# An fp32 operand buffer re-laid so that four batch rows interleave per feature slot, in a DLRM interaction tower

## The reference

```
e = jnp.stack([tbl_0[ids[:, 0]], ..., tbl_25[ids[:, 25]]], axis=1)          # 512 x 26 x 128
combined = jnp.concatenate([dense[:, None, :], e], axis=1)                  # 512 x 27 x 128
interactions = jnp.einsum('bfd,bgd->bfg', combined, combined)
z = concatenate([dense, interactions[:, iu, ju]], axis=1)                   # iu < ju
h = concatenate([z, dense], axis=1)                                         # 607 wide
h = maximum(h @ W_top1 + b_top1, 0);  h = maximum(h @ W_top2 + b_top2, 0);  y = h @ W_top3
```

## Time and profile before

| | |
|---|---|
| median of 3 runs | 181.42 us (180.19 to 184.68) |
| span of the profiled execution | 181.4 us; its own time is not listed apart from the runs |
| mean granted TensorE clock | 0.802 |
| PE / PEld busy | 115.4 us (64%) / 98.3 us (54%) |
| DVE / ACT / POOL busy | 71.7 (40%) / 71.9 (40%) / 79.6 us (44%) |
| DMA | 12.67 MB, mean 70 GB/s |

### The profile page before, as it was taken

One profiled execution on the slowest core, in us unless ns is written; L12 is line 12 of the kernel. 1 busy time (PEld: TensorE's weight loads), 2 busy tenths in 40 slices (PEclk: granted clock), 3 DMA queues, 4 the chain that ended last, 5 costly groups with the idle time before them and its releaser, 6 DMA issues.

```text
span 181.4 us, 1866 instructions
## 1 busy us (share of the span) xinstructions
PE 115.4 (64%) x694; PEld 98.3 (54%) x694; DVE 71.7 (40%) x119; ACT 71.9 (40%) x112; POOL 79.6 (44%) x84
## 2 busy tenths in 40 slices
PE   6177746952814000099889571398785959797795
PEld 6164525832603000078789461197685957797692
DVE  4173476632320011186294400265624643164430
ACT  0465098545042000378664400235541462265422
POOL 1777777777777776073787777000000000000000
PEclk9858975996575555558999955558999999999999
DMA  4956456859831121010112121000000000000000
GB/s 90 260 173 192 150 170 172 186 188 241 251 120 44 44 58 43 14 47 18 54 29 59 46 58 52 20 0 0 4 0 0 0 0 4 0 0 4 0 0 0
DMA packets 5738, 12.67 MB, mean 70 GB/s; under 512 B 1849, under 2 KB 2361, under 8 KB 5602
## 3 DMA queue, kind: packets, MB, share of 16 engines
q1 hardware_dynamic: 3010, 7.26, 13.6%
q0 software_dynamic: 2432, 4.99, 10.3%
q10 hardware_dynamic: 288, 0.32, 0.9%
HBM read 12.55 MB, written 0.00 MB: 69 GB/s over the span
## 4 chain that ended last, share of the span: by engine, by line
PE 46%; another core or an unknown queue 22%; issue 9%; DVE 9%; DMA 7%; ACT 6%; SPq 1%; ACTq 0%; DVEq 0%
PE gram L416 14%; PE late L386 8%; DMA table<-in_tbl 7%; PE late L387 7%; PE gram L432 3%; DVE dots L564 3%; PE look L396 3%; PE late L450 2%; DVE onehot L729 2%; PE late L452 2%; PE late L451 2%; PE look L488 1%; DVE w_lo L803 1%; ACT table_hi L587 1%
## 5 line engine op out<-in xcount | busy, mean ns | idle before, releaser
L341 POOL DMA_INDIRECT e_rows<-in_tbl,idx x76 | 78.8, 1036 | 33.4 <-issue 22.6
L386 PE MATMUL late<-onehot,table_hi 125*128 125x512 f32 x56 | 29.1, 519 | 41.3 <-DVE onehot L729 21.6
L416 PE MATMUL gram<-eT 128*123 128x104 f32 x256 | 35.1, 298 | 11.3 <-issue 8.4
L416 PEld LDWEIGHTS gram<-eT 128*123 128x123 f32 x256 | 33.2, 213 | 12.8 <-issue 9.4
L386 PEld LDWEIGHTS late<-onehot,table_hi 125*128 125x128 f32 x56 | 14.0, 250 | 47.5 <-ACT eT L587 26.1
L729 DVE TENSOR_SCALAR onehot<-ids,row_of_partition 125x512 fp32r<-125x512 int32 x42 | 19.3, 497 | 36.7 <-remote 23.6
L587 ACT ACTIVATE dots<-gram 32x208 f32<-32x208 f32 x32 | 16.5, 517 | 35.3 <-PE gram L416 20.0
L564 DVE COPY dots<-gram 32x208 f32<-32x208 f32 (+1 forms) x32 | 16.5, 516 | 28.7 <-remote 14.9
L387 PE MATMUL late<-onehot,table_lo 125*128 125x512 f32 x56 | 27.2, 486 | 0.0
L607 ACT ACTIVATE onehot<-distance 125x512 fp32r<-125x512 f32 x14 | 8.8, 631 | 27.2 <-remote 24.3
L556 DVE COPY eT<-look 128x512 f32<-128x512 f32 (+1 forms) x12 | 11.7, 972 | 10.8 <-PE look L396 7.5
(11 more groups left out here) (49 smaller groups left out, 109.1 us busy)
## 6 DMA issues: line engine op xcount, KB each, us to landing
table<-in_tbl SPq DMA_DIRECT2D x6, 500.0 KB
ids<-in_ids_bcast SPq DMA_DIRECT2D x6, 256.0 KB
w_raw<-in_w SPq DMA_DIRECT2D x1, 1280.0 KB
e_rows<-in_tbl,idx POOLq DMA_INDIRECT x76
w_raw<-in_w SPq DMA_DIRECT2D x1, 512.0 KB
table<-in_tbl SPq DMA_DIRECT2D x2, 250.0 KB
ids<-in_ids_bcast ACTq DMA_DIRECT2D x1, 256.0 KB
x_rows<-in_dense SPq DMA_DIRECT2D x1, 256.0 KB
```

The costliest lines, as they stand in the source:

```text
L341: pool.indirect_dma_start(out=e_rows[:, t % 2, s, :], out_offset=None, in_=tables[f][:, :], in_offset=bass.IndirectOffsetOnAxis(ap=idx[:, ...
L386: pe.matmul(bank, table_hi[0:KP, i % 2, c, :], hot, start=c == 0, stop=False)
L416: last = pe.matmul(gram[0:ROWS_OUT, n % 2, q, 0:QUADS * NG_COL], eT_flat[:, b * SLOTS:b * SLOTS + ROWS_OUT], eT[:, b:b + QUADS, 0:NG_COL], ...
```

## The change

`eT` becomes [128, 32 blocks of 16 batch rows, 4, 32 slots, 4]. Batch row 16a + 4j + r, slot s, lies at [a, j, s, r]: for one slot, four batch rows are neighbours, and slots are 16 bytes apart. A copy into eT writes four numbers in a row (16 bytes) and then goes on 512 bytes further; before it wrote one number every 128 bytes. A gram product takes the rows with one r out of a block of 16, so its weights and its moving columns are read one number every 16 bytes; before the weights were one run of 123 numbers and the moving operand four runs of 26. Number, shapes and types of all matmuls and copies stay, as do all waits and all DMAs. The four rows of a product are now 4 apart in the batch, and so `turned` writes `pT_hi` and `pT_lo` in runs of four numbers instead of one number every 16 bytes.

```
+RUN = 4
...
-        eT = sb("eT", [P, B, SLOTS])
+        eT = sb("eT", [P, B // 16, QUADS, SLOTS, RUN])
...
-        eT_flat = eT[:, :, :].rearrange("d b s -> d (b s)")
+        eT_run = eT[:, :, :, :, :].rearrange("d g j s r -> d g (j s) r")
...
-                        b = t * P + (c * CHUNK_Q + q) * QUADS
+                        a, r = divmod(t * Q + c * CHUNK_Q + q, RUN)
                         last = pe.matmul(gram[0:ROWS_OUT, n % 2, q, 0:QUADS * NG_COL],
-                                         eT_flat[:, b * SLOTS:b * SLOTS + ROWS_OUT],
-                                         eT[:, b:b + QUADS, 0:NG_COL], start=True, stop=True)
+                                         eT_run[:, a, 0:ROWS_OUT, r],
+                                         eT[:, a, :, 0:NG_COL, r], start=True, stop=True)
...
-            copy(eT[:, t * P:(t + 1) * P, s:s + n].rearrange("d b f -> d f b"),
-                 look[:, LOOK[what] % 2, 0:n * P].rearrange("d (f b) -> d f b", f=n)).then_inc(done, 1)
+            copy(eT[:, t * 8:(t + 1) * 8, :, s:s + n, :].rearrange("d g j f r -> d f (g j) r"),
+                 look[:, LOOK[what] % 2, 0:n * P].rearrange("d (f q r) -> d f q r", f=n, r=RUN)).then_inc(done, 1)
...
-            return [src] + [t[:, k, :].rearrange("p (q j) -> p j q", j=QUADS) for t in (pT_hi, pT_lo)]
+            src = src.rearrange("p j (g r) -> p j g r", r=RUN)
+            return [src] + [t[:, k, :].rearrange("p (g j r) -> p j g r", j=QUADS, r=RUN) for t in (pT_hi, pT_lo)]
...
-                copy(eT[:, :, 1 + NG + i], late[:, LATE["table", i] % 2, :]).then_inc(late_act, 1)
+                copy(eT[:, :, :, 1 + NG + i, :].rearrange("d g j r -> d (g j) r"),
+                     late[:, LATE["table", i] % 2, :].rearrange("d (q r) -> d q r", r=RUN)).then_inc(late_act, 1)
...
-                    copy(eT[:, :, 0], bank)
+                    copy(eT[:, :, :, 0, :].rearrange("d g j r -> d (g j) r"), bank.rearrange("d (q r) -> d q r", r=RUN))
...
-            dve.memset(eT[:, :, NF:SLOTS], 0.0).then_inc(pads_ready, 1)
+            dve.memset(eT[:, :, :, NF:SLOTS, :].rearrange("d g j s r -> d (g j) (s r)"), 0.0).then_inc(pads_ready, 1)
```

## The result

The changed kernel takes **197.42 us** (median of 4 runs, 195.71 to 201.88) against 180.85 (4 runs, 180.19 to 184.68): ratio **1.089**, 95% interval 1.079 to 1.099, so slower by about 16 us. The forecast was 194.1, the range 178 to 203.

The account below looks back on a forecast made before the run. Up to 117 us a stall with slack, not TensorE, was taken to set the time; after it PE's work and hand-overs. 181.4 + 14.9 for strided reads - 2.2 for faster copies = 194.1 us, range 178 to 203.

Parts of the forecast that it names:

- The price of the strided read: Gram passes: PE pays 1.75 ns per number read 16 bytes apart, so 0.222 us a pass, +0.111 at full clock.
- Separate ports, the longer operand sets the pass: Gram passes: weights and moving columns load through separate ports, so 123 weights, not 104 columns, set the time.
- The same rule for neighbours: Gram passes before the change: 123 neighbouring weights at 0.85 ns plus 7 ns give 0.111 us a pass.
- Tiles 2 and 3: Gram tiles 2 and 3, 64 passes each, all on the path: +6.9 and +7.1 us.
- The copies: Copies into eT, pT_hi and pT_lo, after 117 us: writing runs of four goes at neighbours' pace, -2.2 us.
- the cover before 117 us: Stretch to 117 us: its slack hides 96 longer passes of tile 0 and half of tile 1, costed at nothing.
- the sign of being wrong altogether: Before 117 us: a stall that moves by more than 5 us with PE's place in it.
- its sign of being right: Gram tile 1: its second half still starts near 117 us.
- a rival of its own: Stages behind gram tiles: the slower pass lowers PE's clock, so they start cold, up to +8.7 us; chance 0.17.
- its likeliest case: Whole kernel: the forecast's own case, 194.1 us, range 190 to 199, chance 0.40.
- Rival 1: Gram passes: PE's port hides the stride, passes stay 0.111 us, kernel 179.2 us, between 177 and 181.4; chance 0.32.
- The row that spoke against it: Layer-1 passes: fp32r columns at 0.47 ns, 1.9 ns per 16 bytes, no faster than one 16-byte piece in 1.75 ns.

Follow-up runs that it names:

- the series of steps: Kernels whose gram operands are both read at steps of 4, 8, 12, 16 or 32 bytes: 0.111, 0.117, 0.171, 0.230 and 0.235 us a pass.
- reads_tiles01: Kernel before, both gram operands read one number every 16 bytes in gram tiles 0 and 1 only: 186.78 us against 183.33, ratio 1.049.
- weights_run: Changed kernel, but gram weights alone read as neighbours, moving columns still 16 bytes apart: 190.62 us, one run.
- run2: Changed kernel with two batch rows interleaved instead of four: 180.51 us against 182.07 for the kernel before, ratio 0.994; again 178.93 against 180.93, ratio 0.997.
- slot_inner: Kernel before, group copies into eT writing 16 bytes in a row and jumping in PSUM: 177.91 us against 183.33, ratio 0.997; again 178.95 against 180.93, 1.004.
- reads_tiles23: Kernel before, both gram operands read one number every 16 bytes in gram tiles 2 and 3 only: 197.80 us against 183.33, ratio 1.110.

## Why the prediction held, point by point

- **The price of the strided read**, the step on which all hung, was bounded between no extra at all (0.111 us a pass) and 0.40, and taken at 0.222, from strided writes of DVE. It is 0.230 (1.81 ns a number against 1.75). That reads of PE pay about what writes of DVE pay was an argument then; the series of steps shows the price for PE. That it is one and the same limit of the buffer is still only an inference from equal numbers.
- **Separate ports, the longer operand sets the pass**: shown for strided operands by the two kernels with one of them, 0.190 and 0.228 against 0.192 and 0.226. With a shared port each of the two would lie well below the pass in which both are strided (0.230). The same rule for neighbours, 0.85 ns for each of 123 weights, hit 0.111 us but is not shown: the rows had 128 weights in 0.061 us, and the prediction used both numbers. Nothing in the sum hung on it, since the 0.111 us was measured.
- **Tiles 2 and 3**: +6.9 and +7.1 forecast, +7.7 and +7.6 measured, all on the path.
- **The copies**: -2.2 forecast, -2.2 in the changed kernel's chain (1.0, 0.7 and 0.5 in the three places, where 1.0, 0.7 and 0.4 were forecast), -2.1 alone.
- **Mis-sized: the cover before 117 us.** I costed tile 0 and the first half of tile 1 at nothing and the second half at +0.9. The end of tile 1 came 4.2 us later. That much of the loss is covered was right, since the 128 passes alone would be 15 us, but the stall is no fixed wall at 117 us. In the changed kernel ACT and DVE were released at 111.6 instead of 117.0, and then all 64 passes of tile 1 followed at 0.23 us. That is a move of 5.3 us, past the 5 us that the prediction itself had named as the sign of being wrong altogether; its sign of being right, the second half of tile 1 starting near 117 us, failed as well (121.64). The prediction had the stall end with the DMA traffic. In these rows its end goes with a mere pause of POOL's gathers:

```profile
109.69 0.94 POOL L342 DMA_INDIRECT e_rows<-in_tbl,idx  x1 [0.30 <-issue]
111.62 1.03 ACT L589 ACTIVATE dots<-gram 32x208 f32<-32x208 f32 x2 [8.28 <-remote]
113.05 0.56 DVE L557 COPY eT<-look 128x384 f32<-128x384 f32 x1 [0.40 <-remote]
113.28 0.94 POOL L342 DMA_INDIRECT e_rows<-in_tbl,idx  x1 [2.65 <-remote]
```

  In the changed kernel ACT restarts in a gap between two gathers (1.9 us after the start of the one, DMA share down from 0.37 to 0.03 at that moment), DVE's last copy into eT for tile 1 follows, and PE starts 0.1 us behind it, while three more gathers are still to come. In the kernel before the last gather of all starts at 112.84, and ACT restarts at 116.96; in `reads_tiles01` it restarts at 109.00, in a gap from 103.03 to 109.97. Other profiles also have releases amid running gathers (`weights_run` at 103.62), so this is a pattern and not a cause. What the stall is waiting for stays open: no row names it, and its end lies elsewhere in each profile (the transposes behind tile 1 start between 119.9 and 125.9 us in kernels whose passes in tiles 0 and 1 are those of before). It is probably also what makes totals of this kernel scatter: between the two profiles of `run2`'s kernel the start of those transposes differs by 2.3 us, of `slot_inner`'s by 4.8, and the stretch from there to the end by 1.6 and 0.8.
- **Mis-sized: the clock.** It had a rival of its own (0.17, up to +8.7), which came half true. During strided tiles the clock can be at either level: in the changed kernel 17 passes fill 3.9 us at 0.50 and 3.8 us at 1.00,

```profile
113.70:117.60 3.90, 3.89 (x17) 3.90 (x18) 0.50 0.18 49
...
167.20:171.00 3.80, 3.75 (x17) 3.78 (x17) 1.00 0.00 0
```

  so the gram itself hardly cares, as the rival said. But work behind it sometimes runs at 1.2 GHz: +1.4 us in the changed kernel, +4 in `reads_tiles23`. The stage behind tile 1 was at full clock in the changed kernel. The forecast left the clock out of its likeliest case.
- **The total.** +12.7 was forecast. The two profiled executions differ by 18.7, and the missing 6.0 are the cover (+3.3), the size of a pass (+1.3) and the clock (+1.4), all of the same sign. The medians differ by 16.6, as both profiled executions were longer than their medians, by 4.5 and some 2.3 us (an estimate). How near the total came, 194.1 to 197.4, is in part luck: the stall alone moves it by more than that. The prediction also called the span of the profile equal to the median of the runs; the execution of that profile was about 183.2 us long, and the two figures agree by chance. And the range, 178 to 203, reached from no change at all to the slowest case, so the number landing in it says little; the pass, the stages and the copies are what was predicted well.
- **Rival 1**, that PE's port hides the stride, was the one to fear with 0.32, and it fell with the pass of 0.230 us. The row that spoke against it, fp32r columns at 0.47 ns or 1.9 ns for four neighbours, pointed the right way. Whether the buffer sets that pace too, no run shows.

## What to carry to other kernels

A layout that serves the writer of a buffer can cost its reader more: count how many 16-byte pieces each engine touches per number, on both sides. Here 28 copies won 0.3 to 0.5 us each and 256 passes lost 0.12 each at full clock; of the copies' 11.7 us about 2 lay on the path (with those of pT), of the passes' 30 the 15 of tiles 2 and 3 and some 4 of the rest. When an access must jump somewhere, try to let it jump in PSUM: here DVE and ACT read single numbers 512 bytes apart at almost the pace of neighbours, and the kernel that did so in three kinds of copies was the only one that came out clearly faster than the one before.

## What the runs showed of the hardware

- PE reads and DVE and ACT writes of single fp32 numbers in SBUF cost about the same: a PE weight 1.81 ns (steps of 16 bytes), a DVE write 1.75 (steps of 128), an ACT write 0.83 + 0.91 = 1.74 (0.83 is its pace for neighbours: its copies of `pair_rows` in the changed kernel take 406 ns for 288 numbers and 512 for 416).
- A gram pass with a step of 16 bytes takes 0.229 us at 1.2 GHz and 0.224 to 0.230 at 2.4 GHz; one with neighbours 0.206 and 0.111.
- PSUM reads by DVE and ACT show no such price at 512 bytes' distance (689 against 687 ns, and 597 to 630 against 593). The Trainium skill, "Advanced Engine Details and Errata", PSUM Cachelines, warns that non-contiguous PSUM patterns slow matmuls; no run here has a matmul write PSUM so, and for reads of DVE the trace shows no loss (689 against 687 ns).
